# Image loaded ahead of the weights, a projection bias as a row of its weights, and two inverse deviations taken apart

## The reference

```python
pooled = x.reshape(Bb, Cc, n, K, n, K).sum(axis=(3, 5))          # 16 x 16 patches of 12 channels
h = einsum('bcij,ce->bije', pooled, channel_weights)             # 196 tokens
h = concatenate([h, txt], axis=1)                                # 273 tokens
h = h + L0_attn(layernorm(h))      # 12 heads, q, k, v, scores and output rounded to small integers
h = h + L0_ffn(layernorm(h))       # normalises again; 41 tokens chosen by a gate get attention,
                                   # the others a mixed mean; then GELU, 768 wide
h = h + L1_attn(layernorm(h))      # 12 heads, softmax; out @ proj_w.T + proj_b
h = h + L1_ffn(layernorm(h))       # shared expert and 2 of 3 routed ones, SiLU, 384 wide
```

## Time and profile before

| | us |
|---|---|
| runs | 4804.51, 4835.94, 4847.9 |
| median | 4835.94 |
| profiled execution, device time | 4793.07 |
| its span in the profile | 4791.3 |
| TensorE busy | 4135.2 |
| VectorE busy | 2621.2 |
| ScalarE busy | 1759.9 |
| GpSimd busy | 402.3 |
| mean granted clock of TensorE | 0.855 |

### The profile page before, as it was taken

The page is one execution under the profiler, slowest core; times in us unless marked ns, Lnnn a source line. Parts: engine busy times, 40 slices in busy tenths (PEclk is TensorE's granted clock), DMA queues, the critical chain, the costliest instruction groups (busy, mean ns, idle before and its releaser), DMA issues.

```text
span 4791.3 us, 70127 instructions
## 1 busy us (share of the span) xinstructions
PE 4135.2 (86%) x27744; PEld 3228.1 (67%) x27744; DVE 2621.2 (55%) x7217; ACT 1759.9 (37%) x2774; POOL 402.3 (8%) x523
## 2 busy tenths in 40 slices
PE   2779888889888989888889888989889888989888
PEld 1556677676676767677676667767667776766666
DVE  2455555555655555555555655555655555565433
ACT  1234333334333334333334333344433333433332
POOL 2100000000000000000000000000000000000000
PEclk8678888888889888888888888888888888888888
DMA  4111111101111101111101111101111110111000
GB/s 113 31 27 34 32 26 36 33 21 34 32 26 36 33 21 34 32 26 36 33 21 34 32 29 34 36 17 34 36 32 26 36 33 21 34 26 16 13 13 4
DMA packets 154046, 147.13 MB, mean 31 GB/s; under 512 B 64359, under 2 KB 132026, under 8 KB 153722
## 3 DMA queue, kind: packets, MB, share of 16 engines
q1 hardware_dynamic: 153722, 142.64, 14.0%
HBM read 87.28 MB, written 7.91 MB: 20 GB/s over the span
## 4 chain that ended last, share of the span: by engine, by line
PE 62%; DVE 19%; SPq 5%; ACT 5%; DMA 4%; issue 3%; POOL 3%; POOLq 0%; DVEq 0%; ACTq 0%
PE area_a L1034 13%; PE area_n L1042 11%; PE area_b L1034 8%; PE area_m L1042 7%; SPq L457 5%; PE area_n L1259 4%; DMA k1s<-scratch 3%; PE area_n L1066 3%; DVE mx L938 3%; PE area_m L1209 2%; ACT pT_both L666 2%; PE area_a L1117 2%; PE area_b L1057 2%; DVE scratch L949 1%; PE area_m L1066 1%
## 5 line engine op out<-in xcount | busy, mean ns | idle before, releaser
L938 DVE TENSOR_REDUCE mx<-area_n 91x1 f32<-91x273 f32 x1152 | 472.1, 432 | 246.5 <-PE area_n L1259 236.1
L1042 PE MATMUL area_n<-w_dn,hid 128*91 128x192 f32 x2304 | 494.8, 380 | 46.5 <-DVE mrow L943 38.7
L1034 PE MATMUL area_a<-xT,w_gu 96*128 96x273 f32 x1536 | 446.4, 438 | 61.7 <-DVE y L898 38.2
L1042 PEld LDWEIGHTS area_n<-w_dn,hid 128*91 128x91 f32 x2304 | 426.4, 190 | 95.3 <-issue 60.3
L1259 PE MATMUL area_n<-k1s,q1s 96*91 96x273 bf16 x1152 | 350.1, 359 | 152.5 <-DVE mx L938 92.9
L1034 PE MATMUL area_b<-xT,w_gu 96*128 96x273 f32 x1536 | 430.3, 426 | 0.0
L1034 PEld LDWEIGHTS area_a<-xT,w_gu 96*128 96x128 f32 x1536 | 305.0, 208 | 154.2 <-DVE y L898 48.0
L1259 PEld LDWEIGHTS area_n<-k1s,q1s 96*91 96x91 bf16 x1152 | 142.3, 141 | 335.3 <-DVE mx L938 227.2
L1034 PEld LDWEIGHTS area_b<-xT,w_gu 96*128 96x128 f32 x1536 | 313.0, 208 | 73.1
L611 ACT ACTIVATE pa<-area_a,scal 91x820 bf16<-91x820 f32 x192 | 180.3, 939 | 302.3 <-PE area_a L1117 278.2
L949 DVE RECIPROCAL scratch<-area_n 128x273 f32<-128x273 f32 x96 | 179.1, 1866 | 157.1 <-PE area_n L1280 157.1
(11 more groups left out here) (242 smaller groups left out, 7595.4 us busy)
## 6 DMA issues: line engine op xcount, KB each, us to landing
img<-in_x SPq DMA_DIRECT2D x192, 392.0 KB, 3.4
q1s<-scratch SPq DMA_DIRECT2D x192, 102.4 KB, 3.4
k1s<-scratch SPq DMA_DIRECT2D x192, 102.4 KB, 4.4
out<-outb SPq DMA_DIRECT2D x32, 204.8 KB
q0s<-scratch SPq DMA_DIRECT2D x128, 25.6 KB, 3.6
k0s<-scratch SPq DMA_DIRECT2D x128, 25.6 KB, 2.8
pooled<-pooled_dram SPq DMA_DIRECT2D x128, 9.2 KB
tokens<-in_txt SPq DMA_DIRECT2D x32, 57.8 KB
```

Of the source, the lines that this page charges most:

```text
L938: v.tensor_reduce(mx[:, k:k + 1], N[0:TC, k % 2, 0:T], AX.X, ALU.max)\
L1034: last = mm(area[x][0:rows_, j, 0:n], w(j, kc), rhs[:, kc, 0:n], start=(kc == 0), stop=(kc == NK - 1))
L1042: last = mm(by_token(x)[:, c, :], lhs(i, c), w_, start=(i == 0), stop=(i == len(w) - 1))
```

## The change

It has three parts. **First**, the loads are split. SyncE starts with the image. ScalarE, otherwise idle then, issues what the first block needs (`loads`, 38 transfers). What only the second block needs (`later_loads`, 22 transfers: `w_qk1`, `w_v1`, `w_p1`, `b_qk1`, `w_gu`, `w_dn` and the router's) is issued by SyncE at the start of its turn 1, and TensorE, VectorE and ScalarE wait for it at the start of turn 2. VectorE's preparation of the weights moves to the start of its turn 0, behind the six reductions of image 0; ScalarE waits for it at its first `a0`, TensorE at its first `pr0`. **Second**, the second block's projection bias is loaded into row 16 of `w_p1`'s first group, where `oN` is 1; stage `r1`, the semaphore `hb1_ready` and the waits on it go, and `pr1` adds `h1`. **Third**, `inv_std` for `n1s` makes the inverse deviation of `xn2` first, with a power of its own and a semaphore of its own (`twice_ready`), and then that of `y`; `n2n` waits for the one, `n1n` for the other.

```diff
-        load(w_qk1[:, :, :], chan(ins["L1_attn_qkv_w"][:, 0:2 * D]))
+        load_later(w_qk1[:, :, :], chan(ins["L1_attn_qkv_w"][:, 0:2 * D]))
...
-        for i, name in enumerate(("L0_attn_bproj", "L0_ffn_bv", "L0_ffn_bo", "L0_ffn_bf2", None, "L1_attn_proj_b")):
+        for i, name in enumerate(("L0_attn_bproj", "L0_ffn_bv", "L0_ffn_bo", "L0_ffn_bf2", None)):
             src = ins[name] if name else ins["L1_attn_qkv_b"][2 * D:3 * D]
             load(rows[:, i, :], src.partition_broadcast(TC))
+        load(w_p1[HD:HD + 1, 0, :], ins["L1_attn_proj_b"].rearrange("(a n) -> a n", a=1))
...
         @block.sync
         def _(sp):
-            sp.wait_ge(zeroed, 4)
-            with nc.allow_non_contiguous_dma(reason="vectors onto partitions, once"):
-                for dst, src in loads:
-                    sp.dma_start(dst, src).then_inc(weights_in, 16)
             for k in range(NSLOT):
                 sp.dma_start(img[:, k, :], img_dram[0, :, k, :]).then_inc(image_in[k], 16)
 
             def program(t):
+                if t.it == 1:
+
+                    sp.wait_ge(zeroed, 4)
+                    with nc.allow_non_contiguous_dma(reason="vectors onto partitions, once"):
+                        for dst, src in later_loads:
+                            sp.dma_start(dst, src).then_inc(later_in, 16)
...
+                def power(l, k):
+                    return g.tensor_tensor(rstd[l][:, k, :], rstd[l][:, k, :], minus_half[0:TC, 0:NC_], ALU.pow)
+
                 def inv_std(l, stage, of_turn, k, twice=False):
 
                     pool.wait_ge(stats_ready[l], t.image(stage) * of_turn + (k + 1))
                     var = mv[l][:, :, 1]
-                    n = 1
                     if twice:
-                        n = 2
-                        g.tensor_scalar(rstd[l][:, 1, :], var, 1.0 + EPS, EPS * EPS, ALU.mult, ALU.add)
+                        link(g.tensor_scalar(rstd[l][:, 1, :], var, 1.0 + EPS, EPS * EPS, ALU.mult, ALU.add))
+                        power(l, 1).then_inc(twice_ready, 1)
                     link(g.tensor_scalar(rstd[l][:, 0, :], var, EPS, None, ALU.add))
-                    r_ = rstd[l][:, 0:n, :].rearrange("p a c -> p (a c)")
-                    g.tensor_tensor(r_, r_, minus_half[0:TC, 0:n * NC_], ALU.pow).then_inc(rstd_ready[l], 1)
+                    power(l, 0).then_inc(rstd_ready[l], 1)
...
-                    elif stage == "r1":
-                        t.await_last("N", stage, "mx")
-                        if "dy.0" in t.stages:
-                            t.await_taken("N", "dy.0")
-                        add_row(hb1, h1, bproj1).then_inc(hb1_ready, 1)
...
         @block.scalar
         def _(act):
             a = nc.scalar
+            act.wait_ge(zeroed, 4)
+            with nc.allow_non_contiguous_dma(reason="vectors onto partitions, once"):
+                for dst, src in loads:
+                    act.dma_start(dst, src).then_inc(weights_in, 16)
             act.wait_ge(consts_ready, CONSTS)
-            act.wait_ge(weights_ready, 1)
...
             def program(t):
+                if t.it == 2:
+                    act.wait_ge(later_in, 16 * len(later_loads))
...
         @block.vector
         def _(dve):
             v = nc.vector
-            dve.wait_ge(weights_in, 16 * len(loads))
-            dve.wait_ge(consts_ready, CONSTS)
...
             def program(t):
+                if t.it == 0:
+                    prepare()
+                elif t.it == 2:
+                    dve.wait_ge(later_in, 16 * len(later_loads))
...
                     elif name == "n2n":
-                        dve.wait_ge(rstd_ready["B"], n * 2 + 1)
+                        dve.wait_ge(twice_ready, t.done(stage))
                         normal("B", h0, xn2, 1).then_inc(xn_ready["B"], 1)
                     elif name == "n1n":
+                        dve.wait_ge(rstd_ready["B"], n * 2 + 1)
                         link(normal("B", h0, y))
...
                     elif name == "pr1":
                         t.await_full("N", stage)
-                        dve.wait_ge(hb1_ready, t.done(stage))
-                        v.tensor_tensor(hb1[:, :, :], by_token("N"), hb1[:, :, :], ALU.add).then_inc(taken["N"], 1)
+                        v.tensor_tensor(hb1[:, :, :], by_token("N"), h1[:, :, :], ALU.add).then_inc(taken["N"], 1)
```

More of the change, by code:

```diff
@@ L64 @@
 OFFSET.update({x: 1 for x in ("r3 n1s n1n n2n n2f gate k1 v1 rta rtb pk0 gt pk1 s1 t1 c1 ct wo mg n3s n3n n3f f0 fd".split())})
-OFFSET.update({x: 2 for x in "n4s n4n n4f r1 qk1 v2 mx mt a2 pw os ob pr1 n5s n5n n5f rtr".split()})
+OFFSET.update({x: 2 for x in "n4s n4n n4f qk1 v2 mx mt a2 pw os ob pr1 n5s n5n n5f rtr".split()})
 OFFSET.update({x: 3 for x in "cw ey ez dy".split()})
@@ L151, in early_fusion @@
         w_p0 = sb("w_p0", [128, 3, NG, D], BF16)
-        rows = sb("rows", [TC, 6, D])
-        bproj0, bv0, bo, bf2, bv1, bproj1 = [rows[:, i, :] for i in range(6)]
+        rows = sb("rows", [TC, 5, D])
+        bproj0, bv0, bo, bf2, bv1 = [rows[:, i, :] for i in range(5)]
         norm_gb = sb("norm_gb", [KC, 4, NK])
@@ L266, in early_fusion @@
         vector_step, pool_step = sem("vector_step"), sem("pool_step")
[L267 to L268 removed]
+        weights_in, later_in, zeroed, consts_ready, weights_ready = (sem(x) for x in (
+            "weights_in", "later_in", "zeroed", "consts_ready", "weights_ready"))
         image_in = [sem(f"image_in{i}") for i in range(NSLOT)]
@@ L606, in program @@
                     elif name == "a0":
+                        if t.image(stage) == 0 and k == 0:
+                            act.wait_ge(weights_ready, 1)
                         for i, x in enumerate("AB"):
@@ L697, in once @@
                 dve.wait_ge(vector_step, setup[0])
-            for dst, src in ((R_Q, S_Q), (R_K, S_K), (R_V, S_V)):
-                once(v.reciprocal(col(dst), col(src)))
-            once(v.tensor_scalar(col(TMP), col(S_ATT), float(T), None, ALU.mult))
-            once(v.reciprocal(col(TMP), col(TMP)))
-            once(v.tensor_tensor(col(C_P), col(S_Q), col(S_K), ALU.mult))
-            once(v.tensor_scalar(col(C_P), col(C_P), col(TMP), HD ** -0.5, ALU.mult, ALU.mult))
-            once(v.reciprocal(col(TMP), col(S_AFT)))
@@ L715, in _, with prepare @@
-            once(v.tensor_copy(w_p0[:, 2, :, :], w_p0r))
-            v.tensor_copy(col(NOTE), col(TMP)).then_inc(weights_ready, 1)
+            def prepare():
+                dve.wait_ge(consts_ready, CONSTS)
+                dve.wait_ge(weights_in, 16 * len(loads))
+                for dst, src in ((R_Q, S_Q), (R_K, S_K), (R_V, S_V)):
+                    once(v.reciprocal(col(dst), col(src)))
+                once(v.tensor_scalar(col(TMP), col(S_ATT), float(T), None, ALU.mult))
+                once(v.reciprocal(col(TMP), col(TMP)))
+                once(v.tensor_tensor(col(C_P), col(S_Q), col(S_K), ALU.mult))
+                once(v.tensor_scalar(col(C_P), col(C_P), col(TMP), HD ** -0.5, ALU.mult, ALU.mult))
+                once(v.reciprocal(col(TMP), col(S_AFT)))
+                once(v.tensor_tensor(col(C_O), col(S_ATT), col(S_V), ALU.mult))
+                once(v.tensor_tensor(col(C_O), col(C_O), col(TMP), ALU.mult))
+                once(v.tensor_scalar(col(N_BR), col(BR), -1.0, None, ALU.mult))
+                once(v.tensor_copy(w_p0[:, 0, :, :], w_p0f))
+                once(v.tensor_tensor(w_p0r, w_p0f, w_p0[:, 0, :, :], ALU.subtract))
+                once(v.tensor_copy(w_p0[:, 1, :, :], w_p0r))
+                once(v.tensor_tensor(w_p0r, w_p0r, w_p0[:, 1, :, :], ALU.subtract))
+                once(v.tensor_copy(w_p0[:, 2, :, :], w_p0r))
+                v.tensor_copy(col(NOTE), col(TMP)).then_inc(weights_ready, 1)
```

53 lines of the change are left out of this document (24 added, 29 removed).

## The result

| | before | after |
|---|---|---|
| runs beside each other, us | 4804.51, 4818.73, 4835.94, 4847.9 | 4595.77 to 4662.5 (4 runs) |
| median | 4827.33 | **4623.93** |
| profiled execution | 4793.07 | 4622.95 |
| its span | 4791.3 | 4621.2 |
| granted clock, mean | 0.855 | 0.875 |

The ratio after to before is 0.958, 95% interval 0.9535 to 0.9618.

What follows compares the result with a forecast made beforehand. The prediction took TensorE, busy 86% of 4791.3 us, as the bound, with turns partly at a lower clock. Terms -27 - 22 + 0 gave 4744 (profiled) or 4787 (median) us; it forecast 4768 us, range 4700 to 4825.

Steps and rivals of the forecast that it cites:

- The start: Image and early weights first: first statistics at 35.3 instead of 72.03, less a loss in turn 1; -27 us (-34 to -16).
- the loss in turn 1: VectorE waits for image 1's text, issued behind 22 later weight transfers: +10 us, bounds 7.5 and 14.5.
- Part 2: Routed attention's maxima: without GpSimd's bias add VectorE's scaling isn't held; TensorE gains 0.7 us a turn, -22 us (-37 to 0).
- Part 3: First normalisation: two separate powers let xn2 start 0.75 us earlier, taken back by the second power; 0 (-24 to +12 us).
- if the power does the same, it takes back: First normalisation: the second power beside xn2 holds VectorE as an add does, some 0.7 us a turn.
- The rule that the prediction sets against this part: First normalisation: two-port VectorE instructions and any GpSimd instruction exclude each other for the whole instruction; 0 to +12 us.
- the end that it had for this case: First normalisation: a power holds VectorE up not at all, -0.75 us in each of 32 turns, -24 us.
- The sum: Whole kernel: -27 - 22 + 0 gives 4744 us from the profiled execution, 4787 from the median; forecast 4768 us.
- the prediction's own sign of being wrong: Turns changing by more than 1 us either way, which would be the clock and not the work.
- a rival with 0.22: Turns tip into their short kind, 140.1 us instead of 142.8 in 29 turns, -78 us; 4710 us, chance 0.22.
- it gives it back: Turns: the clock rises at the same moment as before, so only the start counts; 4797 us, chance 0.20.

Runs made afterwards that it cites:

- e1_loads_only: The kernel before with only the first part of the change, the split and reordered loads; 4806.23 us.
- e7_add_elsewhere: The changed kernel with the bias add r1 back on GpSimd, placed right behind n3s where VectorE is nearly idle; 4603.71 us.
- e4_one_wait: The changed kernel with xn2 released by the second power instead of the first; 4761.83 us.
- e12_fill_start: e11_both with ten unneeded matmuls of 128 columns on TensorE in its 2.60 us wait ahead of n4f; 4657.81 us.
- e11_both: The changed kernel with xn0 normalised ahead of xn2 and the 22 later weight transfers issued behind image 1's text; 4563.9 us.

## Why the prediction was wrong, point by point

**The start** was right. The weights were there at 31.7 (29, bounds 24 to 35), the first statistics at 38.0 (35.3), the loss in turn 1 was 12.5 us (+10), and the sum of about -21 lies in its range (-34 to -16). e1_loads_only measured 20. By the statistics of image 3 only 16 of it were left in the changed kernel, at the edge of the range; the sum had no term for that.

**Part 2** had the right mechanism and place: the collision went in all turns, and e7_add_elsewhere shows that it was all there was. The direct gain of TensorE, 0.63 us for 0.7, was right too. The size of the term, -22 us with a floor of -37, was wrong: 92 us alone, 135 us in company, since the clock behind the collision wasn't in it.

**Part 3** failed in its step "if the power does the same, it takes back": the second power held up neither normalisation, 0.96 and 0.95 us. The rows it went by were adds of 91 x 576, and they don't carry over to a power of 91 x 3. A nearer one stood in the same trace, xn2 itself beside an add, 2.03 us instead of 0.95 (above), but it is an add too. The rule that the prediction sets against this part, a sum of 0 to +12 us, isn't borne out for this power either; whether these instructions run in a two-port mode no run shows. For the adds it agrees: 1.36 us instead of 0.17, 2.03 instead of 0.95. Taken at the end that it had for this case, -24 us, it would still have been short of the 75 us measured.

**The sum** is where the forecast failed. It priced a wait removed from a turn at its own length. What the runs showed in its place is that length and the low stretch that comes with the wait: 4.7 us a turn for 1.27 us in e4_one_wait. The turns changed by 5.0 us, and the prediction's own sign of being wrong says what that means: "the clock and not the work". I had seen in the earlier trace rows that turns with the same work are of two lengths and that the difference is the clock's, and I made of that a rival with 0.22. It was the main mechanism, and it was also sized too low: I let the turn fall only to the shortest length that the trace before showed, 139.9 us, and it fell to 136.5. The row that could have told was at hand: in the earlier trace rows TensorE waits 2.00 us for the first maximum, and the window behind that wait, from 2105.55 to 2112.30, would have shown the clock at 0.51. Had I laid the low stretches beside the waits ahead of them, I would have asked of each edit which low stretch it removes. One stretch of 6.8 us is worth 3.4 us of work, and times 29 turns that is 99 us for each. (The middle of 4744 and 4787 is 4765.5 and not 4768; that decides nothing.)

The rival "it gives it back" reasoned from the same rows to the opposite, that TensorE stands where it stood if the clock rises at the same moment. The nearest to it is the part of the low stretch that covers another wait, where e12_fill_start got nothing for a higher clock.

## What to carry to other kernels

Where an engine's clock falls at its waits, price a wait by its length and the low stretch behind it: here 1.27 us of delay cost 4.7 us a turn. Before trying to remove one, look for what is waited for during the slow stretch: if the next join would be a wait anyway, the stretch is free, and speeding it up moves it to where it hurts. The add on GpSimd was free or held VectorE for 1.2 us by what VectorE did in that moment, so try such an add's place in the order before rewriting the arithmetic. And don't judge by the mean granted clock of a run: e11_both and e12_fill_start have the same one.

## What the runs showed of the hardware that I had not expected

- Eight matmuls of no use in a 2 us wait of TensorE raised the granted clock behind it from 0.50 to 1.00 (turn 16) and took 75 us from 4824.
- A GpSimd tensor_tensor of 91 x 576 (add) stretched a VectorE tensor_scalar of 123 x 2 from 0.17 to 1.36 us; a GpSimd tensor_tensor of 91 x 3 (power) beside three tensor_scalars of 91 x 192 left them at 0.96 us and took 0.90 to 1.08 instead of 0.85 to 0.88 itself.
- With the same work, a turn of the kernel before, the changed kernel or one with a single part was in 126 of 140 cases within 0.7 us of 136.5, 139.9, 143.4 or 146.8 us, and the parts of the change worked by moving many turns from one of these to another.
